# Head of a second layer prepared during the first layer's experts, and later places for gated adds in a routed stage

## The reference, cut to what matters

```
# layer 0
h = layernorm(x) * (1 + ca) + sa;  x = x + ga * causal_attention(h)
h = layernorm(x) * (1 + cb) + sb
x = x + gb * (h + expert_of(argmax(h @ gate_w.T)) @ h)        # top 1 of 8 experts
# layer 1
h = layernorm(x) * (1 + ca) + sa
n = h / (rms(h) + 1e-8)
u, v = silu(n @ u_w.T + u_b), silu(n @ v_w.T + v_b)
x = x + ga * ((u * toeplitz_mix(v)) @ o_w.T + o_b + h)
h = layernorm(x) * (1 + cb) + sb
n = h * rsqrt(mean(h * h) + eps) * ln_w
x = x + gb * sum over the top 2 of 8 experts of w_e * (silu(n W1a + b1a) * (n W1b + b1b) W2 + b2)
```

## Time and profile before

| what | us |
|---|---|
| three runs | 2402.96, 2402.96, 2404.33 (median 2402.96) |
| the profiled execution | 2401.95 |
| its span | 2400.2 |
| PE busy | 2201.6 (92%) |
| DVE, ACT, POOL busy | 1734.0 (72%), 1309.6 (55%), 948.9 (40%) |
| mean granted PE clock | 0.956 of full |

### The profile page before, as it was taken

The page is one execution under the profiler, slowest core; times in us unless marked ns, Lnnn a source line. Parts: engine busy times, 40 slices in busy tenths (PEclk is TensorE's granted clock), DMA queues, the critical chain, the costliest instruction groups (busy, mean ns, idle before and its releaser), DMA issues. The chain is left out here.

```text
span 2400.2 us, 39193 instructions
## 1 busy us (share of the span) xinstructions
PE 2201.6 (92%) x12976; PEld 1401.9 (58%) x12976; DVE 1734.0 (72%) x2837; ACT 1309.6 (55%) x2549; POOL 948.9 (40%) x1084
## 2 busy tenths in 40 slices
PE   7978999999999999988999689982999999999998
PEld 5852333333333333326777556652788888888887
DVE  7768787878788787825777768864666767666765
ACT  5533777677677777773233244431555555555554
POOL 4652330313121220213555422445355545555555
PEclk9987999999999999998999899985999999999999
DMA  5669035436161711004000100112554545454542
GB/s 202 165 159 120 2 82 107 87 85 116 56 124 53 138 73 39 8 1 137 1 0 0 34 9 18 54 60 92 173 146 136 145 134 160 126 164 124 169 123 51
DMA packets 126583, 220.29 MB, mean 92 GB/s; under 512 B 16448, under 2 KB 92608, under 8 KB 126016
## 3 DMA queue, kind: packets, MB, share of 16 engines
q1 hardware_dynamic: 104368, 173.28, 21.3%
q0 software_dynamic: 22032, 44.64, 13.6%
HBM read 138.83 MB, written 78.67 MB: 91 GB/s over the span
## 5 line engine op out<-in xcount | busy, mean ns | idle before, releaser
L232 DVE TENSOR_REDUCE tile_max<-p_m 128x2 f32<-128x1024 f32 (+1 forms) x628 | 641.8, 1064 | 134.9 <-PE p_m L224 67.5
L1021 ACT ACTIVATE probs<-p_s 128x512 f32<-128x512 f32 (+3 forms) x1280 | 596.2, 534 | 240.0 <-PE p_s L924 234.7
L2300 PE MATMUL p_up<-f_xT,f_w 128*128 128x512 f32 (+1 forms) x2304 | 474.0, 355 | 24.5 <-POOL f_w L2526 12.7
L2300 PEld LDWEIGHTS p_up<-f_xT,f_w 128*128 128x128 f32 x2304 | 370.0, 189 | 85.7 <-issue 26.2
L864 POOL TENSOR_SCALAR_AFFINE_SELECT probs<-probs 128x128 f32<-128x128 f32 x512 | 145.0, 292 | 695.4 <-ACT probs L1021 686.5
L221 PE MATMUL p_m<-ka,qa 96*128 96x512 bf16 (+1 forms) x1256 | 352.5, 363 | 12.8 <-DVE tile_max L232 5.0
L924 PE MATMUL p_s<-qa,ka 99*128 99x512 bf16 (+3 forms) x1280 | 351.7, 351 | 13.3 <-ACT probs L1021 7.1
L2526 POOL TENSOR_TENSOR f_w<-f_raw,f_w 128x1024 fp32r<-128x1024 f32 x95 | 230.9, 2437 | 276.7 <-ACT f_w L2355 276.7
L938 PE MATMUL p_o<-probs,va 128*32 128x512 f32 (+3 forms) x2560 | 300.3, 541 | 0.8 <-issue 0.5
L2315 PE MATMUL p_y<-f_w,f_hidden 128*128 128x256 f32 x1872 | 252.6, 281 | 0.9 <-DVE f_hidden L2453 0.5
L221 PEld LDWEIGHTS p_m<-ka,qa 96*128 96x128 bf16 x1256 | 108.3, 99 | 237.9 <-DVE tile_max L232 135.8
(11 more groups left out here) (279 smaller groups left out, 2724.2 us busy)
## 6 DMA issues: line engine op xcount, KB each, us to landing
x_slots<-mods SPq DMA_DIRECT2D x73, 518.0 KB, 4.2
f_raw<-in_W SPq DMA_DIRECT2D x24, 1024.0 KB, 11.3
f_raw<-in_W1a SPq DMA_DIRECT2D x23, 1024.0 KB, 6.6
f_raw<-in_W1b SPq DMA_DIRECT2D x23, 1024.0 KB, 9.0
qk_scr<-parts SPq DMA_DIRECT2D x48, 256.0 KB, 2.8
qa<-qk_scr POOLq DMA_DIRECT2D x42, 256.0 KB, 15.5
ka<-qk_scr POOLq DMA_DIRECT2D x42, 256.0 KB, 17.3
f_x<-x_slots SPq DMA_DIRECT2D x15, 518.0 KB, 3.8
```

Source lines behind the costliest of these rows:

```text
L232: return nc.vector.tensor_reduce(out=k.tile_max[:, 2 * hp:2 * hp + 2, i, bank], in_=products[:, :, 0:width], op=ALU.max, axis=AX.X)
L1021: nc.scalar.activation(probs[:, (buf * UNITS + n) % NPROBS, h, lo:CH], p_s[:, s_bank(("exp", HG * n + h), buf), lo:CH], ACT.Exp, scale=DH ...
L2300: last = nc.tensor.matmul(p_up[:, f % 2, ab, 0:size], w1[:, wh, ab * KT + kt, f * P:(f + 1) * P], xT[:, t % 2, xh, kt, 0:size], start=(kt, ...
```

## The change

1. `top1_experts`: all 32 tiles are written out, no hardware loop. `center` moves from DVE to ACT (`Identity` with bias -mean/std and scale 1/std, from `minus_means`). `pick` and `finish` are interleaved on DVE (`finish_and_pick`). SP loads layer 1's weights at the start of this block. In each tile one more step (`head`) is added: guarding the gates, adding 1 to ca and cb, and, for the first chunk of each batch (tiles 6 to 16 and 21 to 31), the eleven steps in `STEPS`, so that `xn` of chunks 0 and 1 is ready at the block's end.
2. `layer1`: those parts are gone from its start; the power for 1/std is done in two pieces, over the remaining tiles only.
3. `routed_experts`: `weigh_y` goes from f = 2 to 4, `weigh` from 4 to 5, `gate_of_y` from 5 to 7 (in the last tile 2 and 4), `y_gate` has two buffers; `scatter(t-1)` stays at the end of POOL's tile t where t is ST, but where t is HT it comes after piece 0 of tile t+1; the last tile's y is added, gated and scattered by blocks of 128.

```diff
         def all_tiles(engine, tile):
-            tile(0, 0, 2)
-            tile(1, 1, 2)
-            with engine.Fori(1, NT // 2 - 1) as i:
-                tile(2 * i, 0, 2)
-                tile(2 * i + 1, 1, 2)
-            tile(NT - 2, 0, 1)
-            tile(NT - 1, 1, 0)
+            for t in range(NT):
+                tile(t, t % 2, 2 if t < NT - 2 else NT - 1 - t)
...
+        STEPS = ("spread", "power", "mean", "center", "scale", "shift", "square", "mean_square", "root", "invert", "unit")
+        HEAD_FROM = (6, 21)
+        MODS_AT, GATES_AT = {0: CA, 1: CB}, {2: GA, 17: GB}
...
             # ACT
+                def center(t, par):
+                    act.wait_ge(all_means, 1)
+                    if t >= 2:
+                        act.wait_ge(taken_dve, HALF * (t - 2) + 1)
+                    nc.scalar.activation(h[:, par, :], k.x[:, t, :], ACT.Identity, bias=minus_means[:, t:t + 1],
+                                         scale=k.rstd[:, t:t + 1]).then_inc(h_centered, 1)
...
                 for n, (b, half) in enumerate(halves):
                     act.wait_ge(mod_product, n + 1)
                     nc.scalar.activation(k.mods[1][:, b, 2 * half:2 * half + 2, :], ...).then_inc(mod_copied, 1)
+                center(0, 0)
+                center(1, 1)
                 round_hT(0, 0)
...
             # DVE
+                def finish_and_pick(t, par):
+                    if t:
+                        sum_and_gate(t - 1, 1 - par)
+                    if t < NT - 1:
+                        top_logit(t + 1)
+                    if t:
+                        add_to_x(t - 1, 1 - par)
+                    if t < NT - 1:
+                        equal_to_top(t + 1)
+                    if t:
+                        x_statistics(t - 1)
+                    if t < NT - 1:
+                        first_of_top(t + 1)
+                        one_of_experts(t + 1, 1 - par)
...
-                    if more == 2:
-                        center(t + 2, par)
                     if more:
                         rest_of_hT(t + 1, 1 - par)
-                    if not first(t):
-                        finish(t - 1, 1 - par)
-                    if more:
-                        pick(t + 1, 1 - par)
+                    finish_and_pick(t, par)
+                    head(t)
...
+                    if step == "scale":
+                        dve.wait_ge(head_centered, j + 1)
+                        c_head.step(nc.vector.tensor_tensor(hh, hh, k.mod(1, j, CA), ALU.mult))
+                    if step == "shift":
+                        nc.vector.tensor_tensor(hh, hh, k.mod(1, j, SA), ALU.add).then_inc(k.h_ready, 1)
...
         # layer1, DVE
-                dve.wait_ge(rstd_all, 1)
-                for j in range(B):
-                    center_h(j)
-                for j in range(B):
-                    mean_square_h(j)
-                for j in range(B):
-                    invert(j)
-                guard_gates(nc, k.mods[1], c_own, ...)
         # layer1, ACT
-                for j in range(B):
-                    square_h(j)
-                for j in range(B):
-                    scale_h(j)
...
         # routed_experts
-        WEIGH_Y_AT, HALF_GATE_AT, WEIGHTS_AT, GATE_AT = 2, 4, 4, 5
+        WEIGH_Y_AT, HALF_GATE_AT, WEIGHTS_AT, GATE_AT = 4, 4, 5, 7
+        LAST_WEIGH_Y_AT, LAST_GATE_AT = 2, 4
...
+                        if q == 0 and t >= 2 and SIZES[t - 1] == HT:
+                            scatter(t - 2)
                     if not last_tile(t):
                         gap_exponential(t + 1)
-                    if t:
+                    if t and (SIZES[t] == ST or last_tile(t)):
                         scatter(t - 1)
```

More of the change, by code:

```diff
@@ L1353, in tile, with head @@
                                              ACT.Copy, scale=onehot[:, par, e:e + 1]).then_inc(taken_act, 1)
+                    head(t)
+                def head(t):
+                    j, step = head_at.get(t, (None, None))
+                    if step == "center":
+                        act.wait_ge(head_mean, j + 1)
+                        for u in range(TPC):
+                            row = j * JT + u
+                            last = nc.scalar.activation(k.h[:, 0, j, u, :], k.x[:, row, :], ACT.Identity,
+                                                        bias=minus_mean[:, j, u:u + 1], scale=k.rstd[:, row:row + 1])
+                        last.then_inc(head_centered, 1)
+                    if step == "square":
+                        act.wait_ge(k.h_ready, j + 1)
+                        for u in range(TPC):
+                            if j or u >= 2:
+                                act.wait_ge(k.h_squared, TPC * j + u - 1)
+                            nc.scalar.activation(squares[:, u % 2, :], k.h[:, 0, j, u, :], ACT.Square,
+                                                 accum_out=k.ss[:, 0, j, u:u + 1]).then_inc(k.h_squared, 1)
+                    if step == "unit":
+                        act.wait_ge(k.inv_ready, j + 1)
+                        for u in range(TPC):
+                            nc.scalar.activation(k.xn[:, j, u, :], k.h[:, 0, j, u, :], ACT.Copy, scale=k.inv[:, j, u:u + 1]
+                                                 ).then_inc(k.xn_ready, 1)
                 for n, (b, half) in enumerate(halves):
@@ L1480, in _ @@
                 all_tiles(dve, tile)
[L1481 to L1484, removed]
+                sum_and_gate(NT - 1, 1)
+                add_to_x(NT - 1, 1)
+                x_statistics(NT - 1)
 def layer1(nc, a, k, out):
@@ L2455, in hide @@
                                             ALU.subtract).then_inc(hidden_ready, 1)
-                    if f == WEIGH_Y_AT and t:
+                    if f == (LAST_WEIGH_Y_AT if last_tile(t) else WEIGH_Y_AT) and t:
                         weigh_y(t - 1)
@@ L2471, in weigh_y, with last_y @@
                     rows = y[:, t % 2, 0:blocks, :]
-                    nc.vector.tensor_tensor(rows, rows, y_gate[:, 0:blocks, :], ALU.mult).then_inc(y_ready, 1)
+                    nc.vector.tensor_tensor(rows, rows, y_gate[:, t % 2, 0:blocks, :], ALU.mult).then_inc(y_ready, 1)
+                def last_y(t):
+                    dve.wait_ge(gate_ready_y, t + 1)
+                    dve.wait_ge(down_psum, FB * t + FB)
+                    dve.wait_ge(y_stored, 16 * blocks_to[t - 1])
+                    for u in range(SIZES[t] // P):
+                        row = y[:, t % 2, u, :]
+                        nc.vector.tensor_tensor(row, p_y[:, u, :], b2[:, t % 2, :], ALU.add).then_inc(last_biased, 1)
+                        dve.wait_ge(last_biased, u + 1)
+                        nc.vector.tensor_tensor(row, row, y_gate[:, t % 2, u, :], ALU.mult).then_inc(last_ready, 1)
                 rest_of_x(0)
@@ L2493, in _ @@
                             rest_of_w2(t + 1, f - AHEAD_AT)
-                take_y(NTILES - 1)
-                weigh_y(NTILES - 1)
+                last_y(NTILES - 1)
             @block.gpsimd
@@ L2553, in __init__ @@
         self.scaled, self.x2_ready = m.sem("c_scaled"), m.sem("c_x2_ready")
+        self.bias, self.toep = m.sb("b_uv", [P, 2 * FB1]), m.sb("toep", [P, 3, FB1])
+        self.ss, self.ms, self.rms = (m.sb("l_" + n, [P, 2, 2, TPC]) for n in ("ss", "ms", "rms"))
+        self.inv, self.half = m.sb("l_inv", [P, 2, TPC]), m.sb("l_half", [P, TPC])
+        self.w_loaded = m.sem("l_w_loaded")
+        self.h_ready, self.h_squared, self.h_ms, self.h_rms = (m.sem("l_h_" + n) for n in ("ready", "squared", "ms", "rms"))
+        self.inv_ready, self.xn_ready = m.sem("l_inv_ready"), m.sem("l_xn_ready")
         self.slots = m.sb("slots", [P, 2, NT], U32)
```

212 lines of the change are left out of this document (144 added, 68 removed).

## The result

| | before | after |
|---|---|---|
| median of 4 runs each | 2403.22 | 2434.59 |
| lowest to highest | 2402.96 to 2404.33 | 2434.22 to 2435.85 |
| profiled execution, span | 2401.95, 2400.2 | 2434.36, 2432.5 |

Slower by 1.3%: ratio 1.0131, 95% interval 1.0113 to 1.0148. The forecast of 2419 had the sign right and was 15.6 us short.

The account below looks back on a forecast made before the run. PE, busy 92% of the span, was taken to bound the kernel. Terms -18.4 + 1.1 + 34 - 0.5 = +16.2 gave 2419 against the median; forecast's own range 2408 to 2434, overall 2386 to 2436.

Parts of the forecast that it names:

- The routed stage: Routed experts' half tiles: new PE waits of 4.2 us per half tile, +34 in all, bounds +17 to +47.
- expert block: Expert block: late start, hidden waits and added steps together +1.1 us, bounds -1.6 to +4.
- Layer 1's start: Start of layer 1: `up` comes earlier because `xn` is ready, -18.4 us, bounds -21.4 to -17.7.
- The added steps: Expert block, end of each tile: steps mostly fit DVE's freed time, +2 us, bounds 0 to 4.
- PE's waits, -4.1: Expert block's tiles: PE's listed waits for DVE's low part of the turned tile should go, -4.1 us.
- Gated y at f = 7: Full tile before a half tile: POOL's subtraction interleaves with four DVE products, making `down(13, 0)` late, +2.0 on PE.
- Weighing at f = 4, weights at f = 5: Half tile: 1.2 us taken back at f = 3, later gates delayed, next piece 0 ready at 2012.1, not 2010.96.
- The adds after piece 0: Full tile after a half tile: POOL's four adds delay piece 2, a new PE wait of some 3.1 us.
- the late piece 0 of a half tile: Half tile after two full tiles: piece 0 some 1 us late, taken at nothing; without cover 6 to 8 us.
- DVE keeps the port: Rival, routed stage: DVE's four products run unbroken or DVE catches up, routed term +17, time 2402; chance 0.16.
- the half tiles come out even: Rival, routed stage: moving `weigh_y` frees the chain, piece 0 is 3.1 us earlier, routed term 0, time 2385; chance 0.24.
- The clock falls at the new waits: Rival, routed stage: PE's clock halves after new waits, 5 us each; 2429 at two half tiles, 2459 at all; chance 0.10.

Follow-up runs that it names:

- short piece 2: Head parts plus gated y at f = 7, with POOL subtracting only 8 of 256 columns per group in W1's piece 2 from tile 1: 2373.53.
- split adds: Changed kernel with only the adds moved in the routed stage, two of POOL's four behind piece 0 and two behind piece 2: 2382.94.
- adds late only: Changed kernel with the routed stage's gate and product places put back, leaving the adds behind piece 0 and the last tile by blocks: 2404.60.
- product at f = 1: Head parts with ACT's centring moved ahead and last tile by blocks, plus the product with gated y at f = 1 instead of 2: 2386.81.
- centring earlier: Head parts alone, with ACT's centring of the expert block's first two tiles moved behind its third and fourth modulation copies: 2373.47.

## Why the prediction was right in sign and short in size

The routed stage's +58.4 lies above the upper bound of its term, +47, and the expert block's -4.5 below the lower bound of its own, -1.6. That the whole still ends just inside 2386 to 2436, though not inside the forecast's own 2408 to 2434, is owed in part to these two errors of opposite sign.

*Layer 1's start*, -18.4: right to 0.1, and so was the slow clock behind it (0.92, before 0.91).

*The expert block*, +1.1: it was -4.5. The late transposes (+3.2, measured 3.4) were right; the fall of the clock behind them, 2.2, was missing. The added steps, +2, cost nothing to be seen: the period is 6.48 to 6.50 in all tiles behind the first. The term that was mis-sized is PE's waits, -4.1, taken from the list of waits: some -10 by the tiles' period.

*Gated y at f = 7*: "the same interleaving" came, 3.86, and the short piece 2 shows the cause. The forecast of "+2.0 on PE" holds for this edit by itself: 0.16 + 1.74 = 1.9 in the run with gated y at f = 7 alone. Beside the other edits it is 1.49 + 1.76 = 3.25 at this half tile, 2.4 where one full tile comes before.

*Weighing at f = 4, weights at f = 5*: the step that failed in its mechanism. The 1.2 was taken back as forecast (the wait of 0.79 is gone), but I let "the gate of f = 5" and ACT's rounding be late. The rounding of piece 0 now stands ahead of `weigh`; POOL's subtraction then cuts `weigh`, and the gate product of f = 6 is late. `weigh` was priced at its 1.1 beside an idle POOL. The wait is 2.22 where 1.58 was, in place of a piece 0 that is 1.1 late. That POOL's subtraction is the cause is read from the timeline, where the two end 0.02 apart; no run took POOL's operation away at this place, as the short piece 2 did for gated y.

*The adds after piece 0*: right in place and cause, as the split adds show. By themselves they cost 2.61 (forecast 3.1); in the changed kernel 1.70, since PE is late there already.

*Taken at nothing*: the late piece 0 of a half tile, "6 to 8 us" without cover, cost 1.23 at six half tiles, 7.3: `take_y`'s wait came as well, not instead. And the low part behind POOL's two subtractions, 1.17 for each half tile, stood in no term.

*The rivals.* "DVE keeps the port" and "the half tiles come out even" didn't happen. "The clock falls at the new waits" did, at four half tiles, at 1.5 us each and not 5, and the next wait was shorter by as much; with the adds behind piece 0 and no gate wait ahead of them it cost its 1.5 in full. *The end*, -0.5: it can't be told from nothing.

## What to carry to other kernels

Before moving a small DVE operation that reads two inputs from SBUF, look at what POOL does at the new place: here one of 0.16 us cost 2.35, and four of 0.48 cost 3.9. A change with several parts should be timed part by part: 27 us of gain were hidden under 59 us of loss. The sum of a list of waits can be too small (4.1 where some 10 were to be won); compare the period of a loop too.

## What the runs showed of the hardware that was not expected

POOL operations that are released already follow each other, and a DVE operation with two SBUF inputs can stay outside through all of them. The run with the adds late only shows it in the timelines of POOL and DVE:

```profile
2005.02 7.62 POOL L2649 TENSOR_TENSOR f_w<-f_raw,f_w 128x1024 fp32r<-128x1024 f32 x3
...
2006.90 6.30 DVE L2563 TENSOR_TENSOR f_hidden<-f_gate,f_hidden 128x512 fp32r<-128x512 f32 x1
```

6.30 for an operation that takes 0.69 alone. In the run with the product at f = 1, low parts that came while three such subtractions ran were through in 1.40 and 1.09; this is the first, with ACT's rounding that releases the second subtraction:

```profile
1969.56 1.04 ACT L2464 ACTIVATE f_w<-f_raw 128x1024 fp32r<-128x1024 f32 x1
...
1969.69 1.40 DVE L2563 TENSOR_TENSOR f_hidden<-f_gate,f_hidden 128x256 fp32r<-128x256 f32 x1 [0.48 <-ACT f_hidden L2491]
```

It is not who was ready first: here DVE's operation had waited 0.9 us when the rounding ended at 1970.60, and was through; in the changed kernel the low part of 5.42 had waited as long when the second subtraction was released, and was not. I counted such cases over all traces but that of the short piece 2. In the 178 that were through, POOL's next subtraction had been released 0.2 to 0.5 us before the running one ended; in the 31 that were shut out, 1.2 to 3.6 us before. But the first are all 256 columns wide and the others all 512, so which of the two decides stays open.

The clock's fall doesn't follow the length of the last wait alone: behind the same 2.61 us it fell at four half tiles and not at four others, and at the start of the expert block it fell behind 1.20 us in the run with the centring earlier and not in the kernel before, which has the same 1.20 and a granted clock of 1.00 from 1141 to 1148.
